# Last stage: paired statistics, the tanh addition shared between TensorE and VectorE, and transposes ahead of weight products

## The reference, cut to what matters

```
def step(h, _):
    h = h + 0.01 * tanh(h)
    h = h * sigmoid(h)
    h = layernorm(h, ln_w, ln_b)        # over the 64 channels of a token, eps 1e-5
    h = einsum('bsc,dc->bsd', h, W) + b
    return h
x = scan(step, layernorm(h), 30 times)
h = h + x
```

## The kernel before, in words

| engine | step s, before |
|---|---|
| ACT | th(s), g(s-1), gT(s-4) |
| PE | W(s-5), T(s-4), Y(s) |
| DVE | gn(s-4), statistics(s-2) |
| POOL | var(s-2), rs(s-2) |

## Time and profile before

### The profile page before, as it was taken

The page is one execution under the profiler, slowest core; times in us unless marked ns, Lnnn a source line. Parts: engine busy times, 40 slices in busy tenths (PEclk is TensorE's granted clock), DMA queues, the critical chain, the costliest instruction groups (busy, mean ns, idle before and its releaser), DMA issues. The chain is left out here.

```text
span 2132.7 us, 61654 instructions
## 1 busy us (share of the span) xinstructions
PE 1903.4 (89%) x20166; PEld 1487.2 (70%) x20166; DVE 1674.5 (79%) x4836; ACT 1153.7 (54%) x2296; POOL 484.8 (23%) x431
## 2 busy tenths in 40 slices
PE   2316399999999999999999999999957799999998
PEld 2315277777777777777777777777747477777776
DVE  3205388888888888888888888888865788888887
ACT  0103266666666666666666666666614366666665
POOL 5000000000000000000000000000004699999997
PEclk9999699999999999999999999999987799999999
DMA  3333100000000000000000000000041100000000
GB/s 111 75 71 63 44 3 3 3 3 3 3 3 3 3 3 3 3 3 3 3 3 3 3 3 3 3 3 3 3 95 32 29 0 0 0 0 0 0 0 30
DMA packets 38153, 33.35 MB, mean 16 GB/s; under 512 B 13781, under 2 KB 35477, under 8 KB 37141
## 3 DMA queue, kind: packets, MB, share of 16 engines
q1 hardware_dynamic: 36159, 32.21, 6.4%
q10 hardware_dynamic: 1972, 0.86, 0.2%
HBM read 22.02 MB, written 11.03 MB: 15 GB/s over the span
## 5 line engine op out<-in xcount | busy, mean ns | idle before, releaser
L614 ACT ACTIVATE z1hi<-ps 128x375 f16<-128x375 f32 x820 | 398.7, 486 | 405.1 <-PE ps L556 405.1
L554 PE MATMUL ps<-AThi,y0hi 125*128 125x150 f16 x2460 | 567.1, 241 | 36.5 <-DVE z1lo L650 34.6
L555 PE MATMUL ps<-ATlo,y0hi 125*128 125x150 f16 x2460 | 584.9, 238 | 0.0
L650 DVE TENSOR_TENSOR z1lo<-ps,z1hi 128x375 f16<-128x375 f32 x820 | 445.8, 544 | 171.3 <-ACT z1hi L614 171.2
L556 PE MATMUL ps<-AThi,y0lo 125*128 125x150 f16 x2460 | 564.8, 239 | 0.0
L655 DVE TENSOR_TENSOR y<-ps,negb 125x384 f32<-125x384 f32 x820 | 451.1, 550 | 37.2 <-PE ps L571 37.2
L569 PE MATMUL ps<-W1hi,z1hi 128*128 128x128 f16 x2460 | 455.2, 219 | 0.2 <-DVE y L655 0.2
L571 PE MATMUL ps<-W1hi,z1lo 128*128 128x128 f16 x2460 | 454.1, 219 | 0.0
L570 PE MATMUL ps<-W1lo,z1hi 128*128 128x128 f16 x2460 | 453.6, 219 | 0.0
L645 DVE SCALAR_TENSOR_TENSOR y0lo<-ps,y0hi 125x512 f16<-125x512 f32 x615 | 420.7, 684 | 1.1 <-ACT y0hi L610 1.1
L610 ACT ACTIVATE y0hi<-ps 125x512 f16<-125x512 f32 x615 | 363.4, 591 | 13.4 <-PE ps L536 13.4
(11 more groups left out here) (197 smaller groups left out, 2315.4 us busy)
## 6 DMA issues: line engine op xcount, KB each, us to landing
pooled_parts<-stage SPq DMA_DIRECT2D x410, 4.0 KB
zk<-z_parts SPq DMA_DIRECT2D x16, 360.4 KB
parts<-pooled_parts SPq DMA_DIRECT2D x16, 256.0 KB, 5.7
xs<-in_x_v SPq DMA_DIRECT2D x3, 1201.2 KB
xs<-in_x_v SPq DMA_DIRECT2D x5, 720.7 KB
z_parts<-zp SPq DMA_DIRECT2D x20, 180.2 KB
pooled_parts<-stage SPq DMA_DIRECT2D x205, 2.0 KB
pooled_parts<-stage SPq DMA_DIRECT2D x205, 10.0 KB
```

Source lines behind the costliest of these rows:

```text
L554: nc.tensor.matmul(o, hi, ahi, start=(ph == 0), stop=False, skip_group_check=True)
L555: nc.tensor.matmul(o, hi, alo, start=False, stop=False, skip_group_check=True)
L614: nc.scalar.activation(z1hi[:, q, 0:GV], ps[:, Z1B + q % 2, 0:GV], ACT.Identity).then_inc(z1hi_done, 1)
L650: nc.vector.tensor_tensor(z1lo[:, q, 0:GV], ps[:, Z1B + q % 2, 0:GV], z1hi[:, q, 0:GV], ALU.subtract).then_inc(z1lo_done, 1)
```

## The change

Four things are edited in `feed_forward`.

1. Statistics: one `bn_stats` takes two tokens, with their elements interleaved by the access pattern ("p i d -> p d i"), so that its even moments are one token's and its odd moments the other's. 4 instructions of 128 elements take the place of 8 of 64, and one `tensor_scalar` on 128x8 elements (the sum of squares plus 64 times eps, read with a stride of 3 elements) that of the three joining instructions. POOL's `var` addition is dropped; POOL only takes the power. The waits that guard the buffers move from `parts_done`/`var_done` to `rs_done`.
2. In the first layernorm the mean is read from the same moments, and `sm` goes.
3. The tanh addition of odd chunks moves from PE to DVE: a `scalar_tensor_tensor` x = 0.01 * th + x in the PSUM bank, between `gn` and the statistics of that step. Even chunks keep it on PE. `y_ready` becomes two semaphores.
4. On PE, T(s-4) goes ahead of W(s-5) in each step.

```
-                def body(s, c, on):
+                def body(s, c, on, half):
+                    if on(4):
+                        n, b = s - 4, c % 2
+                        pe.wait_ge(gn_done, n + 1)
+                        if late(n, 2):
+                            pe.wait_ge(gT_done, n - 1)
+                        for j in range(CP):
+                            last = nc.tensor.transpose(ps[:, TB + b, j * P:(j + 1) * P], gn[:, b, j, :], ident[:])
+                        last.then_inc(gT_ready, 1)
                     if on(5):
                         n, cn, b = s - 5, (c - 5) % CH, (c - 5) % 2
                         pe.wait_ge(gT_done, n + 1)
...
-                    if on(4):
-                        n, b = s - 4, c % 2
-                        pe.wait_ge(gn_done, n + 1)
-                        if late(n, 2):
-                            pe.wait_ge(gT_done, n - 1)
-                        for j in range(CP):
-                            last = nc.tensor.transpose(ps[:, TB + b, j * P:(j + 1) * P], gn[:, b, j, :], ident[:])
-                        last.then_inc(gT_ready, 1)
-                    if on(0):
+                    if on(0) and c % 2 == 0:
                         pe.wait_ge(th_done, s + 1)
                         nc.tensor.matmul(ps[:, c, :], pct[:], th[:, c % 2, :], start=False, stop=True,
-                                         skip_group_check=True).then_inc(y_ready, 1)
+                                         skip_group_check=True).then_inc(y_ready[0], 1)
...
+                def statistics(src, pairs, var, b, n, bns, made):
+
+                    for j in range(CP):
+                        last = v_.bn_stats(pairs[:, b, j, :], src[:, 2 * j:2 * j + 2, :].rearrange("p i d -> p d i"))
+                    last.then_inc(bns, 1)
                     dve.wait_ge(bns, n + 1)
-                    v_.tensor_tensor(dm[:, b, :], bs[:, b, :, 1], bs[:, b, :, 4], ALU.subtract).then_inc(diffs, 1)
-
-                    v_.scalar_tensor_tensor(s2[:, b, :], bs[:, b, :, 2], D * EPS, bs[:, b, :, 5], ALU.add,
-                                            ALU.add).then_inc(made, 1)
-                    dve.wait_ge(diffs, n + 1)
-                    v_.scalar_tensor_tensor(q2[:, b, :], dm[:, b, :], D / 4.0, dm[:, b, :], ALU.mult,
-                                            ALU.mult).then_inc(made, 1)
+                    v_.tensor_scalar(var[:, b, :], squares(pairs, b), D * EPS, None, ALU.add).then_inc(made, 1)
...
                         v_.tensor_tensor(gn[:, b].rearrange("p j (i d) -> p (j i) d", i=2), g_[:, cn % NG],
                                          spread(rs[:, b, :], P, CR), ALU.mult).then_inc(gn_done, 1)
+                    if on(0) and c % 2 == 1:
+                        dve.wait_ge(th_done, s + 1)
+                        v_.scalar_tensor_tensor(ps[:, c, :], th[:, c % 2, :], 0.01, ps[:, c, :],
+                                                ALU.mult, ALU.add).then_inc(y_ready[1], 1)
                     if on(2):
                         n, cn, b = s - 2, (c - 2) % CH, c % 2
                         dve.wait_ge(g_done, n + 1)
                         if late(n, 2):
-                            dve.wait_ge(parts_done, 2 * n - 2)
-                        for r in range(CR):
-                            last = v_.bn_stats(bs[:, b, r, :], g_[:, cn % NG, r, :])
-                        last.then_inc(bn_done, 1)
...
+                            dve.wait_ge(rs_done, n - 1)
+                        statistics(g_[:, cn % NG], bs, var, b, n, bn_done, var_done)
```

More of the change, by code:

```diff
@@ L1142, in feed_forward @@
         gT = sb("gT", [P, 2, CP * P])
[L1144 to L1149, removed]
+        bs, bs0 = (sb(f"bn_pairs{i}", [P, 2, CP, 6]) for i in range(2))
         var, var0 = (sb(f"var64_{i}", [P, 2, CR]) for i in range(2))
@@ L1165, in feed_forward @@
         th_done = sem("th_done")
-        y_ready = sem("y_ready")
+        y_ready = [sem("y_ready_by_tensor"), sem("y_ready_by_vector")]
         g_done = sem("g_done")
         bn_done = sem("bn_done")
-        diff_done = sem("diff_done")
-        parts_done = sem("parts_done")
         var_done = sem("var_done")
@@ L1183, in steps, with squares, means @@
                     before(s)
-                body(s, s, lambda lag, s=s: s - lag >= 0)
+                body(s, s, lambda lag, s=s: s - lag >= 0, lambda lag, s=s: (s - lag) // 2)
             with eng.Fori(1, ITERS) as it:
                 for c in range(CH):
-                    body(it * CH + c, c, lambda lag: True)
+                    body(it * CH + c, c, lambda lag: True, lambda lag, c=c: it * (CH // 2) + (c - lag) // 2)
             for s in range(N, N + LAG):
-                body(s, s - N, lambda lag, s=s: 0 <= s - lag < N)
+                body(s, s - N, lambda lag, s=s: 0 <= s - lag < N, lambda lag, s=s: (s - lag) // 2)
         def late(n, k):
             return not isinstance(n, int) or n >= k
+        def squares(pairs, b):
+            return pairs[:, b].rearrange("p j (i k) -> p (j i) k", i=2)[:, :, 2]
+        def means(pairs, b):
+            return pairs[:, b].rearrange("p j (i k) -> p (j i) k", i=2)[:, :, 1]
         out_rows = out.rearrange("b s d -> (b s d)").rearrange("(c p n) -> c p n", c=CH, p=P)
@@ L1208, in _ @@
                 pool.wait_ge(expo_made, 1)
[L1210 to L1214, removed]
                 def first(c):
                     if c < CH:
-                        pool.wait_ge(parts0_done, 2 * c + 2)
+                        pool.wait_ge(var0_done, c + 1)
                         if c >= 2:
                             pool.wait_ge(x0_ready, c - 1)
-                        inverse_roots(s20, q20, var0, rs0, c % 2, c, var0_done, rs0_done)
+                        nc.gpsimd.tensor_tensor(rs0[:, c % 2, :], var0[:, c % 2, :], expo[:], ALU.pow).then_inc(rs0_done, 1)
                 first(0)
-                def body(s, c, on):
+                def body(s, c, on, half):
                     if on(2):
                         n, b = s - 2, c % 2
-                        pool.wait_ge(parts_done, 2 * n + 2)
+                        pool.wait_ge(var_done, n + 1)
                         if late(n, 2):
                             pool.wait_ge(gn_done, n - 1)
-                        inverse_roots(s2, q2, var, rs, b, n, var_done, rs_done)
+                        nc.gpsimd.tensor_tensor(rs[:, b, :], var[:, b, :], expo[:], ALU.pow).then_inc(rs_done, 1)
                 steps(pool, body, lambda s: first(s + 1))
@@ L1241, in body @@
                         if late(s, 2):
-                            act.wait_ge(y_ready, s - 1)
+                            act.wait_ge(y_ready[c % 2], half(2) + 1)
                         nc.scalar.activation(th[:, c % 2, :], ps[:, c, :], ACT.Tanh).then_inc(th_done, 1)
@@ L1245, in body @@
                         n, cn = s - 1, (c - 1) % CH
-                        act.wait_ge(y_ready, n + 1)
+                        act.wait_ge(y_ready[cn % 2], half(1) + 1)
                         if late(n, NG):
@@ L1291, in _ @@
             def _(dve):
-                def statistics(bs, dm, s2, q2, b, n, diffs, made, bns):
+                def statistics(src, pairs, var, b, n, bns, made):
+                    for j in range(CP):
+                        last = v_.bn_stats(pairs[:, b, j, :], src[:, 2 * j:2 * j + 2, :].rearrange("p i d -> p d i"))
+                    last.then_inc(bns, 1)
                     dve.wait_ge(bns, n + 1)
-                    v_.tensor_tensor(dm[:, b, :], bs[:, b, :, 1], bs[:, b, :, 4], ALU.subtract).then_inc(diffs, 1)
-                    v_.scalar_tensor_tensor(s2[:, b, :], bs[:, b, :, 2], D * EPS, bs[:, b, :, 5], ALU.add,
-                                            ALU.add).then_inc(made, 1)
-                    dve.wait_ge(diffs, n + 1)
-                    v_.scalar_tensor_tensor(q2[:, b, :], dm[:, b, :], D / 4.0, dm[:, b, :], ALU.mult,
-                                            ALU.mult).then_inc(made, 1)
+                    v_.tensor_scalar(var[:, b, :], squares(pairs, b), D * EPS, None, ALU.add).then_inc(made, 1)
@@ L1303, in centre @@
                 def centre(c):
                     b = c % 2
+                    rows = h2[:, c, :].rearrange("p (r d) -> p r d", d=D)
                     dve.wait_ge(h2_loaded, (c + 1) * 16)
                     if c >= 2:
-                        dve.wait_ge(var0_done, c - 1)
-                    for r in range(CR):
-                        last = v_.bn_stats(bs0[:, b, r, :], h2[:, c, r * D:(r + 1) * D])
-                    last.then_inc(bn0, 1)
-                    statistics(bs0, dm0, s20, q20, b, c, diff0, parts0_done, bn0)
@@ L1313, in centre @@
[L1313 to L1317, removed]
+                        dve.wait_ge(rs0_done, c - 1)
@@ L1319, in first @@
+                        dve.wait_ge(centred, c - 1)
+                    statistics(rows, bs0, var0, b, c, bn0, var0_done)
+                    v_.tensor_tensor(x0c[:, b, :].rearrange("p (r d) -> p r d", d=D), rows,
```

(1 more changed line is left out.)

3 lines of the change are left out of this document (removed).

## The result

The changed kernel takes 2153.54 us (median of 6 runs, 2140.96 to 2157.82) against 2135.14 us (6 runs, 2131.40 to 2143.71). The ratio is 1.0069 with a 95% interval of 1.0043 to 1.0096: slower by about 15 us, between 9 and 20. (It is taken over all runs; the two medians alone lie 18 apart.) The forecast was 2141, slower, with a range of 2117 to 2152. On the scale of the first three runs the ratio gives 2150, between 2145 and 2156, near the upper end of the range; the median of the changed kernel's own runs lies 1.5 above that end.

The account below looks back on a forecast made before the run. PE was taken to bound the old kernel, and a ring of waits through DVE the changed one. Loop +3.2, start +3.8 and end -1.2 summed to +5.8 us, span 2138.5, median 2141 us, range 2117 to 2152.

Parts of the forecast that it names:

- PE as the bound before: In the old loop PE alone sets the pace: 2.41 us a pass, 4.813 a pair.
- The ring: Loop, from one even step's `gn` over T, W, th, the DVE addition and statistics to the next: 4.85 us per pair.
- step 1: The ring's first term: `gn` 0.69, 0.05 to PE's weight load, 0.11 to the matmul, together 0.85 us.
- Its being closed by edits 3 and 4 together: W stands behind T, T waits for `gn` on DVE, and DVE's odd addition waits for th: a closed chain, 4.85 us.
- Terms of DVE: DVE per pair: four paired `bn_stats` 0.86, wait 0.05, small operation 0.09, PSUM addition 0.60; 3.8 us in all.
- the dear operations (0.07): Rival: DVE statistics at 1.10 and addition at 0.69 make the ring 5.18, time 2170; chance 0.07.
- The loop's sum: From th(7) to th(179), 86 pairs at 4.85 instead of 4.813 us: +3.2 us.
- The rival of a shorter ring (0.20): Ring shorter than PE's old pace, deciding at 4.78 per pair; time 2121 or 2105; chance 0.20.
- The variance held by a power: DVE's new variance may wait for POOL's power: 4.62 a pair, nothing in the loop, up to 0.8 us at the start.
- Start and end: Last stage outside the loop: start to th(7) +3.8 us (+2.5 to +5), end after th(179) -1.2 (-2 to 0).
- PE as the bound after (0.04): Rival: PE still bounds the changed loop at 3.95 us per pair, -74 us, time 2064; chance 0.04.
- the clock (0.03): Rival: PE's idling lowers its clock, the ring gains 1.7 us a pair, up to +146, time 2282; chance 0.03.

Follow-up runs that it names:

- experiment 3: Only the cheaper statistics and first-layernorm mean (edits 1 and 2), all tanh additions on PE, W ahead of T; 0.9977 of the kernel before.
- experiment 9: Edits 1, 2 and 4 without 3: cheaper statistics, T ahead of W, every tanh addition on PE; 0.9978 of the kernel before.
- Experiment 5: Changed kernel with edits 1 and 2 undone: old statistics back, shared tanh addition and T ahead of W kept; 1.0312 of the kernel before.
- experiment 1: Changed kernel with edit 4 undone, so W(s-5) stands again ahead of T(s-4) on PE; 1.0016 of the kernel before.
- experiment 2: Changed kernel with the odd addition on DVE behind the statistics of its step instead of ahead; 0.9648 of the kernel before.
- experiment 8: Changed kernel with the odd addition behind the statistics on DVE and W ahead of T on PE; 1.0008 of the kernel before.
- experiment 4: Changed kernel with the hardware loop's body holding two iterations (twelve steps), leaving 14 back edges of 29; 1.0033 of the kernel before.

## Why the prediction was right, point by point

- **PE as the bound before.** Right: experiments 3 and 9 change nothing in the loop (413.9 and 413.5).
- **The ring.** Right in mechanism and nearly in size: 4.775 measured, 4.85 said. Most of the difference is step 1: from `gn`'s end to T's start 0.06 instead of 0.16. A T that waits has its weight load at 1893.12 and its matmul at 1893.13, where the earlier trace rows have 0.11 between them; T then takes 0.05 more. Experiment 5 adds 0.51 to the statistics and gets 0.50 a pair.
- **Its being closed by edits 3 and 4 together.** Right, and with a second half that the prediction lacked. It said that T ahead of W closes the ring, and not what would stand there without it: experiment 1 shows another ring of 4.81, over gT. Edit 4 is needed for any gain. The place of the addition on DVE is what spoiled it (experiments 2 and 8).
- **Terms of DVE.** Paired `bn_stats` 0.278 said, 0.282 measured; four 0.86 and 0.88; the small instruction 0.09 and 0.08; the wait with one semaphore 0.05 and 0.03; the addition into PSUM 0.60 apart said, 0.61 measured, single 0.70. Cost by element was right, which kept the dear operations (0.07) out.
- **The loop's sum.** +3.2 said, +9.7 measured, and what failed is a term that isn't in the sum. By the ring alone it would be 86 x (4.775 - 4.813) = -3 us; the back edges between th(7) and th(179) add 28 x 0.46 = +13. I took the loop for an even stream, as it had been under PE's pace (413.95 = 172 x 2.4067, with the same branches in it). The long pairs vanish in experiments 1 and 8, where PE isn't full either but the ring runs over PE and ACT, and get half as many in experiment 4. So the edge costs where the ring passes DVE. Why DVE loses 0.38 to 0.48 us there wasn't tested. The two errors, -6.5 for the hops and +13 for the edges, partly cancelled, and the loop was 6.5 us off.
- **The rival of a shorter ring (0.20).** Its condition came true: it asked for a ring shorter by 0.07, and the ring was 0.075 shorter, by the hops and not by a cheaper `bn_stats`. The back edges, which no case of the prediction had, hid it. Without their 13 us the stage would have been 1 us longer instead of 14.1, which counts as the same and not as slower by the prediction's own limit of 4.3. So that the direction came out was luck.
- **The variance held by a power.** Not so. `var` at 1893.90 took 0.17 while POOL worked on two powers from 1892.63 to 1896.16; 62 of the 186 ran wholly inside a power, and none of the 186 took over 173 ns. The rule that the Trainium skill gives in "SBUF — State Buffer", section "Who interferes with whom", would hold a two-port TENSOR_SCALAR for the whole of a GpSimd instruction that came first; L344 in the earlier trace rows agrees with it. These 62 weren't held; whether they ran in a two-port mode no trace shows. If they had been held, the start would have been up to 0.8 longer by the prediction, for which I had taken a half.
- **Start and end.** End -1.2 said, -1.4 measured; without the shared addition T ahead of W is worth 2.7 there (experiment 9 against 3). Start +3.8 said, +5.9 measured. Up to X(4) the working was right: it has X(4) 25.3 us into the stage, and it came at 25.2. The miss lies behind it, in the level of the clock (the 3.4 us from W(0) to W(1) are given without a working). I had counted X(4), Y(4) and X(5) at the upper level, 1.02 + 0.69 + 0.86 + 0.86 = 3.43 us to T(1); they took 1707.42 - 1701.52 = 5.90, X(4) and Y(4) 2.08 each, with a granted clock of 0.66 on average over the window 1700 to 1710:

```profile
1704.29 2.08 PE L1272 MATMUL ps<-th,pct 128*128 128x512 f32 x2
...
1706.15 1.43 PE L1250 MATMUL ps<-x,ident 128*128 128x512 f32 x2
...
1707.42 0.60 PE L1260 MATMUL ps<-ident,gn 128*128 128x128 f32 x4
```

- **PE as the bound after (0.04) and the clock (0.03).** PE waits for `gn`; the clock stayed at 1.00 in the loop with PE 84% busy. In the start it did cost, as above.

In all +5.8 was said and +14.1 measured in the stage. The mechanism of the ring was right, and its size to 0.08 us. That the kernel became slower came from the back edges, which the sum had at nothing, and from the start.

## What to carry to other kernels

When work moves from a full engine to another, list what the receiving engine does behind the moved instruction, and follow the chain back to that engine: here an addition ahead of a block of statistics or behind it made 84 us of difference, with the same load on every engine. A move frees time only if every ring is shorter than the old pace, and so two orders may have to change together (0.965) where each alone gives nothing (1.002, 1.001, 1.007). And a fixed cost of an engine that nobody waited for, such as DVE at its loop's back edge here, can come to be paid once a ring runs over that engine.

## What the runs showed of the hardware

- A `bn_stats` over 128 elements with its two tokens interleaved by stride costs 282 ns, against 211 for 64 elements: 1.1 ns per element more, near the 1.03 of contiguous elements, and so hardly a penalty for alternating between two tokens 256 bytes apart.
- DVE wrote a 128x512 float32 result into PSUM while reading it from there in 696 ns, the same as an SBUF result (692), next instruction after 0.61.
- A back edge cost 0.46 us in the changed kernel (0.38 on DVE and 0.08 on PE), where the ring ran over DVE. It was 0.58 with the old statistics and 0.52 with the first additions on PE, both in a body of six passes, and 0.55 in a body of twelve. Nothing of it can be seen where the ring ran over PE and ACT alone or where PE was full with its old order (413.95 us with 28 of them).
